# Eight planes of expert sums in place of four: plain scatters only, the planes merged between the experts, and layer 1's preparation moved to experts 2 and 3

## The reference

```python
scores = jax.nn.softmax(xt @ Wr, axis=-1)
G, idx = jax.lax.top_k(scores.T, k)            # N = 4096 tokens, E = 8 experts, k = 1024 each
X_in = xt[idx]
h = jax.nn.gelu(jnp.einsum('ekd,edh->ekh', X_in, W1) + b1[:, None, :], approximate=False)
X_e = jnp.einsum('ekh,ehd->ekd', h, W2) + b2[:, None, :]
contrib = (G[..., None] * X_e).reshape(E * k, D)
out = jnp.zeros((N, D)).at[idx.reshape(-1)].add(contrib)
...
x = x + gb * out
```

## Time and profile before

| | |
|---|---|
| median of 3 runs | 1176.46 us (1174.49 to 1183.04) |
| the profiled execution | 1176.31 us, of which the span from the first to the last instruction is 1174.3 us |
| busy shares of the span | PE 80%, DVE 70%, ACT 56%, POOL 36% |
| mean DMA rate | 90 GB/s over the span |

### The profile page before, as it was taken

One profiled execution on the slowest core, in us unless ns is written; L12 is line 12 of the kernel. 1 busy time (PEld: TensorE's weight loads), 2 busy tenths in 40 slices (PEclk: granted clock), 3 DMA queues, 4 the chain that ended last, 5 costly groups with the idle time before them and its releaser, 6 DMA issues. The chain is left out here.

```text
span 1174.3 us, 24926 instructions
## 1 busy us (share of the span) xinstructions
PE 936.6 (80%) x8605; PEld 642.8 (55%) x8605; DVE 816.6 (70%) x1708; ACT 656.4 (56%) x2201; POOL 419.4 (36%) x334
## 2 busy tenths in 40 slices
PE   6779898898999989898671479878618889885885
PEld 3456666575666656575570456555404555553664
DVE  4777776869687786867468755212447687879997
ACT  2476575867768686867425234232116788873432
POOL 2332442433333233333100187778830223222111
PEclk9898999999999999999955679998958999997888
DMA  7665454453635444454220213325950000000000
GB/s 209 160 174 145 112 129 111 125 134 99 160 101 140 107 125 130 118 142 102 69 73 5 74 49 87 87 72 113 234 154 1 1 2 2 1 2 0 28 19 27
DMA packets 102148, 106.27 MB, mean 90 GB/s; under 512 B 19264, under 2 KB 71984, under 8 KB 102080
## 3 DMA queue, kind: packets, MB, share of 16 engines
q1 hardware_dynamic: 94400, 96.74, 30.7%
q0 software_dynamic: 7680, 8.66, 3.7%
HBM read 30.68 MB, written 16.99 MB: 41 GB/s over the span
## 5 line engine op out<-in xcount | busy, mean ns | idle before, releaser
L857 POOL TENSOR_TENSOR qk_cos<-qk_raw,const 128x512 f32<-128x512 f32 x128 | 182.6, 1427 | 302.5 <-ACT qk_raw L609 302.5
L595 ACT ACTIVATE prob<-psS,neg_max 128x96 f32<-128x96 f32 x512 | 167.9, 342 | 77.8 <-DVE neg_max L690 76.7
L456 PE MATMUL psQ<-a_xnT,weights 128*128 128x512 f32 x250 | 145.1, 664 | 2.7 <-ACT a_xnT L641 2.0
L564 PEld LDWEIGHTS psO<-probT,v_windows 96*64 96x64 f32 x2048 | 70.8, 138 | 138.1 <-ACT probT L669 116.1
L705 DVE TENSOR_TENSOR qk_roped<-qk_cos,qk_swapped 128x512 f32<-128x512 f32 x128 | 121.5, 949 | 0.3
L564 PE MATMUL psO<-probT,v_windows 96*64 96x64 f32 x2048 | 88.6, 229 | 40.4 <-ACT probT L669 40.0
L595 ACT ACTIVATION_READ_ACCUMULATOR prob<-psS,neg_max 128x1 f32 x512 | 105.1, 205 | 0.0
L696 DVE TENSOR_TENSOR qk_swapped<-qk_swapped,const 128x512 f32<-128x512 f32 x128 | 91.4, 714 | 19.2 <-DMA qk_swapped<-qk_raw 18.3
L1522 POOL DMA_INDIRECT ex_rows<-rows,ex_index x64 | 67.9, 1061 | 100.1 <-DMA ex_index<-lists 81.5
L669 ACT COPY probT<-psT 96x512 f32<-96x512 f32 x128 | 76.8, 600 | 46.7 <-PE psT L544 46.7
L609 ACT COPY qk_raw<-psQ 128x512 f32<-128x512 f32 x125 | 74.1, 593 | 41.8 <-PE psQ L456 41.7
(11 more groups left out here) (352 smaller groups left out, 1952.3 us busy)
## 6 DMA issues: line engine op xcount, KB each, us to landing
qk_swapped<-qk_raw SPq DMA_DIRECT2D x512, 64.0 KB, 2.0
v_windows<-v_tok SPq DMA_DIRECT2D x32, 384.0 KB, 4.4
v_windows<-v_tok SPq DMA_DIRECT2D x32, 256.0 KB, 3.6
sums<-zeros SPq DMA_DIRECT2D x32, 256.0 KB, 2.5
mod<-mod_rows SPq DMA_DIRECT2D x12, 512.0 KB, 7.1
ex_w<-in_L_ffn_W SPq DMA_DIRECT2D x16, 256.0 KB, 3.1
v_windows<-v_tok SPq DMA_DIRECT2D x32, 96.0 KB, 2.1
rows<-rt_h SPq DMA_DIRECT2D x8, 256.0 KB, 2.4
```

What stands on the lines that cost most here:

```text
L456: last = nc.tensor.matmul(bank, k.wqkvT[:, col:col + P], xnT[:, :], start=True, stop=True)
L564: ins = nc.tensor.matmul(psO[D * j:D * j + D, i * P + a * HALF:i * P + (a + 1) * HALF], vw[:, par, a, t, hd], probT[:, 2 * j + i, a * HALF ...
L595: last = nc.scalar.activation(prob[:, s, 2 * j + i, :], psS[:, s, j, i * KW:(i + 1) * KW], ACT.Exp, bias=nmax[:, s, 2 * j + i:2 * j + i + ...
L857: nc.gpsimd.tensor_tensor(rcos[:, half, :], raw[:, half, :], k.const[:, K_COS:K_COS + T], ALU.mult).then_inc(cos_done, 1)
```

## The change

There are eight planes. Expert e scatters with plain writes into plane e, so the adding form and its wait are gone. SP still zeroes planes 0 to 3 in attention (32 DMAs, now as 2 KB runs in place of 512 B runs). ACT zeroes planes 4 to 7 at the start of its router stream with 8 DMAs of 1 MB, on its own DMA queue, beside SP's stores of h. `zeros` is now held for the whole program, and SP waits for all of them at the router's end.

The planes are merged as they come: behind the weights of e+2 (and its index, which stands ahead of them) SP waits for expert e-1's scatters and loads plane e-1 in two halves of 1 MB; plane 0 goes to `k.total`, the others to `k.spare`, each half only when the merge of the plane before has read it. DVE adds plane e-2 behind expert e's y (`merge`, 8 adds), from expert 3 on, and planes 5 and 6 behind expert 7. Plane 7 is loaded in three pieces as before, the first two into a separate piece of memory (`k.late`). Layer 1's modulation is multiplied out behind expert 2, its weights are turned behind expert 3, and its store and spreads go out in SP's stream behind expert 3.

```diff
@@ SP in attention
-                sp.dma_start(k.sums[plane].rearrange("(b t p) c -> b p t c", t=TILES, p=P)[b], zeros[:, :, :]).then_inc(cleared, 16)
+                sp.dma_start(k.sums[plane].rearrange("(b p t) c -> b p t c", t=TILES, p=P)[b], zeros[:, :, :]).then_inc(cleared, 16)
@@ phase_router, scalar
+            for plane in range(PLANES // 2, PLANES):
+                for half in range(2):
+                    act.dma_start(k.sums[plane][half * B // 2 * T:(half + 1) * B // 2 * T].rearrange("(b p t) c -> p b t c", t=TILES, p=P),
+                                  k.zeros[:, :, :].unsqueeze(1).to_broadcast([P, B // 2, TILES, C])).then_inc(rest_stored, 16)
@@ phase_experts, tensor
-                if last_pair and e == E0 - 2:
-                    mod.turn(pe)
-                    mod.multiply(pe)
...
-                if last_pair and e == E0 - 1:
+                if e == 2:
+                    mod.turn(pe)
+                    mod.multiply(pe)
+                if e == 3:
                     pe.wait_ge(mod.rows_ready, 1)
                     weights1.tensor(pe)
@@ phase_experts, sync
+            def load_plane(plane):
+                half = B // 2
+                for lo in (0, half):
+                    wait(sp, k.merged, B * (plane - 2) + lo + half)
+                    sp.dma_start((k.spare if plane else k.total)[:, lo:lo + half, :, :].rearrange("p b t c -> p (b t) c"),
+                                 k.sums[plane][lo * T:(lo + half) * T].rearrange("(t p) c -> p t c", p=P)).then_inc(k.plane_ld[lo // half], 16)
...
                     index_of(e + 2, par, turn + 1)
                     weights(e + 2, par)
-                if last_pair and e == E0 - 2:
+                if e == 3:
                     mod.store(sp)
                     mod.spread(sp, range(MODS), k.mod_rest[1])
-                    sp.wait_ge(scattered[0], 16 * SLOTS * 3)
-                    load_plane(0, k.total)
-                    sp.wait_ge(scattered[1], 16 * SLOTS * 3)
-                    load_plane(1, k.spare)
+                if e >= 1:
+                    sp.wait_ge(scattered[1 - par], 16 * SLOTS * ((e - 1) // 2 + 1))
+                    load_plane(e - 1)
                 if last_pair and e == E0 - 1:
-                    sp.wait_ge(scattered[0], 16 * SLOTS * 4)
-                    sp.wait_ge(k.merged, B)
-                    load_plane(2, k.spare)
                     sp.wait_ge(scattered[1], 16 * SLOTS * 4)
                     for i, (lo, hi) in enumerate(((0, 1), (1, 2), (2, B))):
-                        sp.wait_ge(k.merged, B + (1 if i < 2 else 2))
+                        if i == 2:
+                            sp.wait_ge(k.merged, B * (PLANES - 2))
...
@@ phase_experts, gpsimd
-                if e >= PLANES:
-                    pool.wait_ge(scattered[par], 16 * SLOTS * (turn + 1 - PLANES // 2))
...
-                    nc.gpsimd.indirect_dma_start(k.sums[e % PLANES], bass.IndirectOffsetOnAxis(ap=index2[:, par, n:n + 1], axis=0),
-                                                 y[:, par, n, :], None, compute_op=ALU.bypass if e < PLANES else ALU.add).then_inc(scattered[par], 16)
+                    nc.gpsimd.indirect_dma_start(k.sums[e], bass.IndirectOffsetOnAxis(ap=index2[:, par, n:n + 1], axis=0),
+                                                 y[:, par, n, :], None).then_inc(scattered[par], 16)
@@ phase_experts, vector
+            def merge(plane):
+                wait(dve, k.merged, B * (plane - 1))
+                for b in range(B):
+                    if b % (B // 2) == 0:
+                        dve.wait_ge(k.plane_ld[b // (B // 2)], 16 * (plane + 1))
+                    nc.vector.tensor_tensor(k.total[:, b, :, :], k.total[:, b, :, :], k.spare[:, b, :, :], ALU.add).then_inc(k.merged, 1)
...
+                if e == 2:
+                    mod.finish(dve)
+                if e == 3:
+                    weights1.take(dve)
+                if e >= 3:
+                    merge(e - 2)
                 if last_pair and e == E0 - 1:
-                    weights1.take(dve)
...
+                    merge(e - 1)
```

More of the change, by code:

```diff
@@ L37 @@
 ROW = C + E0
-PLANES = 4
+PLANES = 8
 H1 = 2
@@ L354, in phase_attention0 @@
         ymul = sb("y_mul", [P, TILES, C])
-        zeros, zeroed, cleared = sb("zeros", [P, TILES, C]), sem("zeroed"), sem("cleared")
+        zeros, zeroed, cleared = k.zeros, sem("zeroed"), sem("cleared")
         psS = ctx.enter_context(nc.psum_tensor("psS", [P, 2, 2, 512], F32))
@@ L953, in _ @@
             sp.wait_ge(ld_late, 16 * 3)
-            sp.wait_ge(cleared, 16 * B * PLANES)
+            sp.wait_ge(cleared, 16 * B * PLANES // 2)
 def phase_router(nc, k):
@@ L987, in phase_router @@
             sem(f"rt_{n}") for n in ("h_ready", "h_turned", "hs_ready", "logit", "logit_out"))
-        h_stored, scores_ready, scores_stored = [sem(f"rt_h_stored{i}") for i in range(2)], sem("rt_scores"), sem("rt_scores_stored")
+        h_stored, scores_ready, rest_stored = [sem(f"rt_h_stored{i}") for i in range(2)], sem("rt_scores"), sem("rt_rest_stored")
         shifted, exp_done, counted, totals, ranked, count_ready = (
@@ L1107, in _ @@
             sp.wait_ge(scores_ready, 1)
-            sp.dma_start(k.rows.rearrange("(n p) c -> p n c", p=P)[:, :, C:ROW], s[:, :, :]).then_inc(scores_stored, 16)
+            sp.dma_start(k.rows.rearrange("(n p) c -> p n c", p=P)[:, :, C:ROW], s[:, :, :]).then_inc(rest_stored, 16)
             for s2 in range(2):
                 sp.wait_ge(h_stored[s2], 16 * B // 2)
-            sp.wait_ge(scores_stored, 16)
+            sp.wait_ge(rest_stored, 16 * (1 + PLANES))
         @block.vector
@@ L1471, in index_of @@
                 sp.dma_start(index[:, par, :], k.lists[e].rearrange("(p s) -> p s", s=SLOTS)).then_inc(index_ld[par], 16)
-            def load_plane(plane, out):
-                sp.dma_start(out.rearrange("p b t c -> p (b t) c"),
-                             k.sums[plane].rearrange("(t p) c -> p t c", p=P)).then_inc(k.plane_ld[plane], 16)
+            def load_plane(plane):
[4 more added lines that the diff above has]
+                                 k.sums[plane][lo * T:(lo + half) * T].rearrange("(t p) c -> p t c", p=P)).then_inc(k.plane_ld[lo // half], 16)
             weights(0, 0)
@@ L1614, in body @@
             def body(e, par, turn, first, last_pair):
-                if last_pair and e == E0 - 2:
-                    mod.finish(dve)
                 if not (last_pair and e == E0 - 1):
@@ L1632, in body @@
                     weights1.quantise(dve)
-                if last_pair and e == E0 - 1:
-                    weights1.take(dve)
-                    dve.wait_ge(k.plane_ld[0], 16)
-                    dve.wait_ge(k.plane_ld[1], 16)
-                    for b in range(B):
-                        nc.vector.tensor_tensor(k.total[:, b, :, :], k.total[:, b, :, :], k.spare[:, b, :, :], ALU.add).then_inc(k.merged, 1)
-                    dve.wait_ge(k.merged, B)
-                    dve.wait_ge(k.plane_ld[2], 16)
-                    for lo, hi in ((0, 2), (2, B)):
-                        nc.vector.tensor_tensor(k.total[:, lo:hi, :, :], k.total[:, lo:hi, :, :], k.spare[:, lo:hi, :, :], ALU.add).then_inc(k.merged, 1)
+                if e == 2:
[4 more added lines that the diff above has]
+                    merge(e - 2)
+                if last_pair and e == E0 - 1:
+                    merge(e - 1)
             take(0, 0, 0)
@@ L2029, in add_experts @@
                 gb = k.mod0[:, GB, b, :].unsqueeze(1).to_broadcast([P, TILES, C])
-                last = k.spare[:, b, :, :]
+                last = (k.late if b < 2 else k.spare)[:, b, :, :]
                 dve.wait_ge(own.sem, own.mark(nc.vector.tensor_tensor(mul[:, :, :], k.total[:, b, :, :], last, ALU.add)))
@@ L2106, in _ @@
             own.turn(0)
-            dve.wait_ge(k.merged, B + 2)
+            dve.wait_ge(k.merged, B * (PLANES - 2))
             dve.wait_ge(k.sums_ld[0], 16)
@@ L2180, in build @@
         k.x = sb("x", [P, B, TILES, C])
+        k.zeros = sb("zeros", [P, TILES, C])
         k.const = sb("const", [P, K_END])
@@ L2194, in build @@
         k.mod, k.mod1 = sb("mod", [P, MODS, B, C]), sb("mod1", [P, MODS, B, C])
-        k.spare = k.mod[:, 0:PLANES, :, :].rearrange("p m b c -> p (m b c)").rearrange("p (b t c) -> p b t c", t=TILES, c=C)
-        k.plane_ld = [ctx.enter_context(nc.semaphore(f"plane_ld{i}")) for i in range(PLANES - 1)]
+        k.late = k.mod[:, CB, :, :].rearrange("p b c -> p (b c)").rearrange("p (b t c) -> p b t c", t=TILES, c=C)
+        k.spare = k.mod[:, SA:CB, :, :].rearrange("p m b c -> p (m b c)").rearrange("p (b t c) -> p b t c", t=TILES, c=C)
+        k.plane_ld = [ctx.enter_context(nc.semaphore(f"plane_ld{i}")) for i in range(2)]
         k.merged = ctx.enter_context(nc.semaphore("merged"))
```

2 lines of the change are left out of this document (1 added, 1 removed).

## The result

The changed kernel takes **1193.32 us** (median of 4 runs, 1191.47 to 1193.61), the kernel before 1175.47 us beside it (4 runs, 1173.98 to 1183.04). The ratio on record is 1.0126, with a 95% interval of 1.0091 to 1.0162: slower by 1.3% (the two medians alone, from four runs each, would give 1.0152). The forecast was 1179.0 with a range of 1164 to 1198, and a chance of 0.3 for slower by over 1%: the time lies in the range, on the side that I held for the less likely. It is 14 us above the forecast itself and above the 1173 to 1188 that I gave the forecast's own mechanism; the range reached so far only for the sake of rival 2, which did not come. That the range holds the time is in part luck.

The account below looks back on a forecast made before the run. POOL, running gathers and scatters back to back, was taken to set the experts' pace. From 1176.3 us, -10.8 (scatters, contention and tail), +5.5 (late index) and +8.0 (router zeros) gave 1179.0 us, range 1164 to 1198.

Parts of the forecast that it names:

- rival 2: Router: stores of h queue behind all the zeros, sequence 2 starting 20 to 33 us later; 1191 to 1204 us, chance 0.25.
- the forecast's own mechanism: Router and experts: index of expert 6 late and stores of h stretched; 1173 to 1188 us, chance 0.5.
- The scatters: Experts 4 to 7 on POOL: plain scatters save 18.0 us, of which 4.5 us come ahead of the last gather.
- The tail: Last y to layer 1: planes 5 and 6 merged, plane 6 landing in 10.3 to 10.8 us; layer 1 starts at 856.1.
- The index: Before gather 6: expert 6's index lands behind store, spreads and plane 2, so POOL waits; +5.5 us, bounds 0 and 9.
- late landings of gathered rows are hidden in the middle: Middle experts: gathered rows landing up to 3.2 us later cost nothing, since scatters start well after y is ready.
- The router: Router loop: ACT's zeros make stores of h land in 5.6 us, so DVE waits; +8 us, bounds 0 and +33.
- issuing the eight costs ACT some 0.5 us each: hidden: Router start: ACT's issue of eight zeroing DMAs costs nothing, since ACT is first needed six microseconds into the block.
- the zeros are nearly free: Router: zeros cost only 0 to 3 us; 1172 us with the late index, 1166.5 without; chance 0.2.
- Contention at expert 7: Expert 7's gathers: plane 4's load delays their landing by half of 3.2 us, taken as 1.5 us; last y at 839.0.
- The merges cost nothing: Experts: merging planes 1 to 4 takes DVE 4.95 us each, in gaps where it waited for gathered rows; no cost.
- the third rival: Experts: a merge waiting for its plane holds up DVE's take of the next expert; 0 to 3 us, chance 0.05.

Follow-up runs that it names:

- d_before_plain: The kernel before, with plain scatters for experts 4 to 7 into planes 0 to 3 and without their wait, sums left out: 1173.81 us, ratio 0.996.
- b_index_first: The changed kernel, with the index of expert e+3 loaded right behind the weights of e+2: 1184.66 us, ratio 1.0047.
- e_act_busy: a_zeros_late, with 22 copies that nothing reads on ACT where its zeroing DMAs stood: 1184.9 us, ratio 1.006.
- c_both: The changed kernel with the edits of a_zeros_late and b_index_first together: 1176.33 us, ratio 0.997.
- g_plane_held: c_both, with SP waiting until expert 7's rows have landed before it loads plane 4: 1169.8 us, ratio 0.9926; repeated 1168.14 us, ratio 0.993.
- i: g_plane_held, with each of a merge's 8 adds waiting until the one before has finished: 1166.84 us, ratio 0.9914.
- a_zeros_late: The changed kernel, with planes 4 to 7 zeroed by SP behind the store of the scores instead of by ACT: 1183.53 us, ratio 1.0041.

## Why the prediction was right where it was, and wrong where it was not

**The scatters: right.** 1.03 us each as foreseen, and of 18 us only expert 4's share counts ahead of the last gather. d_before_plain gives 4.7 for the 4.5. In the changed kernel 2.5 of it is left; 1.6 of the missing 2.0 is the first gather of expert 6, which takes 2.62 us there beside a merge.

**The tail: right.** 17.5 us from the last y to layer 1 against the 17.8 of the working (its 856.1 less the start of that y), and 17.5 to 18.1 in all eight-plane kernels. It went as foreseen: plane 6's load starts when the merge of plane 5 has read half of its buffer (868.80), and its second half is there at 878.91, 10.1 us later, against 10.3 to 10.8. This is the larger gain of the change, about 8 us.

**The index: right in its mechanism, sized at half.** POOL waits in front of gather 6 with the index as releaser, and b_index_first takes that away. Gather 6 came 11.7 us late, not 5.5. From the start of the spreads to gather 6 the forecast had 21.7 us; it took 23.3 (779.18 to 802.52), 1.6 more. The other 4.6 us are a late start of the spreads: 97.6 us behind the first gather, where the forecast had 93.0. Here a step failed: I wrote that late landings of gathered rows are hidden in the middle, and let the store go only some 1.1 us later for PE's sake. They are hidden from POOL, but not from PE. Plane 0's load goes out beside the gathers of expert 3 and plane 1's (754.09) beside those of expert 4, and PE waits for the rows of both:

```profile
743.17 1.09 PE L1400 MATMUL ex_psX<-const,ex_rows 128*128 128x128 f32 x8 [2.27 <-DMA ex_rows<-rows,ex_index]
...
766.87 1.09 PE L1400 MATMUL ex_psX<-const,ex_rows 128*128 128x128 f32 x8 [2.92 <-DMA ex_rows<-rows,ex_index]
```

It is the second wait that stands right in front of expert 3's down-projection: expert 4's rows come 7.1 us behind its last gather, 1.5 before. Without that wait PE would still have been 2.4 us later there than before, mainly from the first wait and from 3.2 us of layer 1's modulation (752.98 to 756.19). The down-projection of expert 3 so ends 3.7 us later behind the first gather than before (some 1 us was foreseen), SP's weights of expert 5 wait for it, and everything behind them in SP's stream with them. The last 1.5 us lie between the store and the spreads, 3.2 us (776.00 to 779.18) where I took 1.7. No run holds planes 0 and 1 back, so this chain is read from the rows and not tested; two traces with the same program up to there, the kernel before and d_before_plain, differ by 1.2 us in expert 3's y.

**The router: mechanism right, +10.4 in place of +8.** Two terms were off, and their delays ran beside each other. A store of h lands in up to 9.2 us, not 5.6, so that DVE waits 10.6 us for three of them. And the step "issuing the eight costs ACT some 0.5 us each: hidden" failed: only the first two took that, the eight took 15.06 us. By itself that costs the router 2.3 us (e_act_busy). How the 10.4 is shared when both are there isn't told apart by these runs; DVE's waits name the stores alone. The rival in which the stores stand behind all of the zeros did not come: sequence 2 starts at 595.35, not 612, and a store issued in the middle of the zeros lands before they are done. The one in which the zeros are nearly free did not come either. The Trainium skill's rule that an engine goes round robin between queues ("DMA: Bandwidth & Descriptors", Queues, rings and completion order) had given an estimate of 3.5 us more for a store; the trace has up to 6.8 more, so the rule as I used it falls short here. I had counted every row of 512 B as a packet; in that section of the Trainium skill a packet is some 9 to 17 descriptors, so that the 3.5 us hold only if the packets of both queues have equally many.

**Contention at expert 7: right in kind, too small.** I took half of 3.2 us, since plane 4's load runs beside half of the gathers. The rows land 4.0 us later than before, and the last y is 3.6 us late. It isn't a matter of the share: a load that starts 0.65 us ahead of the last gather's end makes the rows 3.2 us later than before (d_before_plain), one that starts 2.0 us ahead 3.9 us (c_both), and one that starts behind it nothing (g_plane_held). In the kernel before, the DMA engines were near full only from 822 to 851 us (share 0.97, against 0.51 from 790 to 822), that is behind expert 7's gathers (804 to 814) and not beside them.

**The merges cost nothing: wrong.** DVE's `take` is nowhere late by them in the changed kernel, so the third rival did not come. I looked only at DVE, where it is true. On POOL a gather is held beside each of the first two merges, for 3.9 us at expert 5 and 1.6 at gather 6. In the changed kernel itself the first lies ahead of the wait for the index and costs no time; in c_both and g it does, 3.65 us by i. The price that this rival had on record, 0 to 3 us, was for DVE; POOL was not in it.

**The start of the experts, +1.6 us, is none of the change's.** PE's 31 ranking matmuls there took 1.94 us before and 3.53 us after. c_both and g_plane_held have the same program up to there, and take 3.53 and 1.94 us. PE's granted clock tells them apart: over these matmuls it was 1.00 in the kernel before and in g_plane_held, the upper of its two levels (2.4 GHz), and 0.51 in the changed kernel and 0.50 in c_both, the lower one (1.2 GHz). In six of the traces the clock rose 1.4 to 2.4 us ahead of the first of them, and the stage is 56.2 to 56.5 us; in the other six it rose 2.7 to 3.8 us behind it, and the stage is 57.8 to 58.1. Since the same program shows both, the 1.6 us are not put down to the change.

The sum, then: 8.0 was 10.4, 5.5 was 11.7, -10.8 was -7.0 (-2.5, +3.6, -8.1), and +1.6 and -1.6 elsewhere cancel. The terms that were off all erred one way: wherever two streams of transfers met, I took the nearest row or half of it, and each meeting cost more than that.

## What to carry to other kernels

Before a big transfer is put into an in-order stream, list the small ones behind it on that engine and who waits for them; a 4 KB index behind 5 MB held the pacing engine for 8 us, and sending it one turn earlier costs nothing. Put megabytes where no engine waits for a landing (the search for thresholds took 8 MB of zeros for nothing, the loop beside it paid 10 us), and hold a bulk load back until the last gather that matters has landed (4 us at expert 7). An engine's free time is not the only price of moving work onto it: the eight adds were free on VectorE and held GpSimd for 4 us, until they had gaps.

## What the runs showed that I had not expected

- **Issuing DMAs can itself take long.** On ACT's queue 1 MB DMAs took 0.46 us to issue and then up to 3.40 us each; the same eight issued by SP (a_zeros_late) took up to 3.01 us each, and the issue of a small index behind big loads took SP 3.78 us, 0.33 without them. No run here shows where the limit lies.
- **Adds of two SBUF tiles without a gap on VectorE can hold one GpSimd DMA instruction** until the last of them is done (4.7 to 5.8 us in ten traces), and adds that start 0.73 us apart in place of 0.60 did not. Why it happens at the first merge in those ten traces and hardly at later ones, where GpSimd's instructions beside the adds mostly took 0.9 to 1.5 us, and not beside the adding scatters of the kernel before, stays open.
- **Expert 7's gathered rows land in 1.6 us or in 4.3 to 5.9 us**, by whether megabytes on SP's queue are under way when its last gather ends. At the experts before it such transfers give 2.7 to 7.1 us, so the delay has no fixed size.
